# Cross-attention and ternary feed-forward: the first tile's rows in another order, four raw weight pieces, and staging moved

## The chip, the cores and the metric

The kernel runs on one core of a Trainium2 chip. The metric is the device time of one execution in microseconds (us). A core has TensorE (PE; its weight loads are PEld), VectorE (DVE), ScalarE (ACT), GpSimd (POOL), SyncE (SP) and 16 DMA engines. All five run their own instruction streams and meet at semaphores.

## The reference

```python
def layernorm(x): return (x - x.mean(-1)) / sqrt(x.var(-1) + 1e-5)

# x, ctx: (8, 256, 256) f32; mask: (8, 256) int; weights are ternary, -1, 0 or 1, with a scale for each output
def xattn(q, ctx, mask):
    s = einsum('bqd,bkd->bqk', q, ctx) / sqrt(256)
    s = where(causal_upper | (mask == 0), -inf, s)
    return einsum('bqk,bkd->bqd', softmax(s), ctx)

def ffn(x):                                   # tlin(x, w, s) = (x @ w.T) * s
    h = silu(tlin(x, w1, s1)) * tlin(x, w2, s2)   # 256 -> 1024
    h = gelu(tlin(h, h1, sh1))                    # 1024 -> 1024
    h = gelu(tlin(h, h2, sh2))                    # 1024 -> 1024
    return tlin(h, w3, s3)                        # 1024 -> 256

x = x + xattn(layernorm(x), ctx, mask)
x = x + ffn(layernorm(x))
```

## The kernel before

**Tiles.** The 2048 tokens are four tiles of 512 (two batches of 256), a tile is four rows of 128 tokens, numbered 0 to 3; rows 0 and 1 are batch 0. An odd row attends to 256 keys, an even one to 128.

**Arithmetic.** Products in the feed-forward run in F32R, a form of fp32 in which TensorE needs one pass. So that the result stays exact, the activations are split in a high part (`xn_hi`, `h_hi`, rounded to F32R) and a low part (`xn_lo`, `h_lo`), and each weight block is multiplied with both. Weights may run in F32R only if their low 16 bits are zero.

**Weights, pieces and flags.** The weights are 22 pieces of 128 x 1024 f32 (512 KB): 0 to 3 gate and up (two chunks of 128 outputs each), 4 to 11 the first hidden layer, 12 to 19 the second, 20 and 21 the last. A piece is first copied from DRAM to DRAM (`stage`, the form with large packets), then from there to SBUF (`load_piece`). In tile 0, ScalarE sums the low 16 bits of each piece (`test_piece`, L391), TensorE adds the sums over the partitions (`sum_flag`, L968), VectorE writes the flag (`take_flag`, L690), and a `segment` on TensorE reads the flag and runs its products in F32R or in F32. The last flag, LAST, covers pieces 17 to 21. `sum_flag(flag)` waits on TensorE until all tests up to the flag's last piece are done:

```python
pe.wait_ge(low_summed, end)
nc.tensor.matmul(flag_bank(flag), ones[:], low_sums[:, first:end], start=True, stop=True).then_inc(flag_mm, 1)
```

**Raw pieces.** Pieces 0 and 1 are needed too early for the round trip. They are loaded straight into `gate` and `residual` (`load_raw`, L263), tested there, and GpSimd copies them as F32R into `h_hi[1]` (`first_weights`, L366). They are loaded again in the usual way for the later tiles.

**The head.** The first tile's attention has code of its own, row by row, with an order written out by hand on each engine (the lists at the end of each engine's block). Rows are taken as 1, 0, 3, 2 (`FIRST_ROWS`). For each row: statistics of x (VectorE, L615, L620), deviation (L625, or ScalarE L403), turned by TensorE (L1055), copied as queries (L632, L410), scores (L1073) on top of a mask that TensorE has put in the bank (`first_mask_in`, L1063, L1065), maximum (L639), exponentials (ScalarE L417), turned (L1082), copied (L653, L424), attended (L1092), added to x (L666), statistics again, reciprocal square root on GpSimd (`rstd_of`, L337, L338), normalised (L677), turned (L1100), split (ScalarE L430, VectorE L684). `stay_busy` (L1047) issues products whose result is not used.

**The first tile's products.** Gate and up for chunks 0 to 2 are done by batch (256 columns), chunks 3 to 7 in full (512 columns), all at L907. Then the two hidden layers (L928), into which the attention of the next tile is woven, and the last layer (L947). Tiles 1 to 3 follow the same way.

**The queue.** SyncE issues nearly all DMAs of the kernel, in program order, and a wait holds what stands behind it. After the head it alternates `load_piece(n)`, which waits until `stage(n)` has landed, and `stage(n + 2)`.

## Time and profile before

| | |
|---|---|
| median of 3 runs | 376.17 us (375.77 to 377.38) |
| profiled execution | 376.71 us, span 374.6 us |
| TensorE, VectorE, ScalarE, GpSimd busy | 97%, 47%, 40%, 8% of the span |
| DMA | 34.15 MB, 91 GB/s over the span |

The span runs from the first to the last instruction of the profiled execution; its own time is 2.1 us more. Timeline rows give start, duration, engine, line, operation and tiles; where several of one kind follow each other they are merged and the duration is that of the whole stretch. "idle before <- releaser" is how long the engine stood still and what ended it. In the chain of waits each piece of time belongs to the work that the end was waiting for.

### The profile page before, as it was taken

How to read it: one execution, taken by the hardware profiler on the slowest of the kernel's cores; microseconds unless marked ns; L12 is line 12 of the kernel's file. 1: busy time of each engine (PE TensorE's matmuls, PEld its weight loads, DVE VectorE, ACT ScalarE, POOL GpSimd, SP SyncE). 2: the span in 40 equal slices, each digit the busy share in tenths (PEclk: the TensorE clock that was granted, in tenths of full speed). 3: DMA queues.
4: the chain of work that ended last, by engine and by line, in shares of the span. 5: the costliest groups of instructions: out<-in, count | busy, mean ns of one | idle time of the engine just before them, and what ended most of it. 6: DMA issues, size and time to landing. Idle time of an engine off the chain costs nothing.

```text
span 374.6 us, 4879 instructions
## 1 busy us (share of the span) xinstructions
PE 364.7 (97%) x1797; PEld 306.8 (82%) x1797; DVE 176.9 (47%) x406; ACT 149.3 (40%) x252; POOL 28.5 (8%) x50
## 2 busy tenths in 40 slices
PE   8898999999999999999998999999999999999996
PEld 5676888888898888888888888888889888888886
DVE  2747652334565745234564665232456563232324
ACT  3678766593134632262130653235113473122120
POOL 7300031000100022000010004000010000000000
PEclk9999999999999999999999999999999999999999
DMA  7989998981411000000141000000000100000001
GB/s 260 335 288 366 380 401 281 317 274 70 173 40 46 3 2 2 2 0 3 59 139 60 2 1 3 0 2 3 2 0 30 32 3 2 2 2 2 2 2 58
DMA packets 10499, 34.15 MB, mean 91 GB/s; under 512 B 1522, under 2 KB 4468, under 8 KB 10100
## 3 DMA queue, kind: packets, MB, share of 16 engines
q1 hardware_dynamic: 10448, 33.45, 24.9%
q8 instruction: 39, 0.64, 0.7%
q14 instruction: 8, 0.07, 0.1%
q10 hardware_dynamic: 4, 0.00, 0.0%
HBM read 31.34 MB, written 13.63 MB: 120 GB/s over the span
## 4 chain that ended last, share of the span: by engine, by line
PE 93%; issue 2%; ACT 1%; DVE 1%; POOL 1%; DMA 1%; DVEq 0%; ACTq 0%
PE ring L928 62%; PE ring L907 14%; PE ring L947 8%; PE att L858 2%; PE att L877 2%; PE att L848 1%; DMA mask<-in_mask 1%; ACT scaled L391 1%; PE ring L1073 1%; ACT gate L468 1%; PE att L866 1%; PE ring L1055 0%; ACT h_hi L458 0%; PE ring L1092 0%; POOL rstd L338 0%
## 5 line engine op out<-in xcount | busy, mean ns | idle before, releaser
L928 PE MATMUL ring<-h_hi,weights 128*128 128x512 f32 x512 | 201.5, 394 | 0.1
L928 PE MATMUL ring<-h_lo,weights 128*128 128x512 f32 x512 | 199.5, 390 | 0.0
L928 PEld LDWEIGHTS ring<-h_hi,weights 128*128 128x128 f32 x512 | 96.2, 188 | 19.9 <-issue 0.2
L928 PEld LDWEIGHTS ring<-h_lo,weights 128*128 128x128 f32 x512 | 96.2, 188 | 19.7
L480 ACT ACTIVATE act<-ring,scales 128x512 f32<-128x512 f32 x64 | 44.1, 689 | 155.8 <-PE ring L928 155.8
L716 DVE CAST h_hi<-act 128x512 fp32r<-128x512 f32 x64 | 27.3, 427 | 147.9 <-ACT act L480 134.1
L610 DVE TENSOR_TENSOR h_lo<-act,h_hi 128x512 fp32r<-128x512 f32 x96 | 66.2, 689 | 2.6
L907 PE MATMUL ring<-xn_hi,weights 128*128 128x512 f32 x112 | 43.7, 390 | 1.5 <-issue 1.5
L907 PE MATMUL ring<-xn_lo,weights 128*128 128x512 f32 x112 | 43.6, 389 | 0.0
L468 ACT ACTIVATE gate<-ring,scales 128x512 f32<-128x512 f32 x32 | 22.1, 690 | 37.6 <-PE ring L907 37.6
L703 DVE SCALAR_TENSOR_TENSOR act<-ring,scales,gate 128x512 f32<-128x512 f32 x32 | 24.0, 751 | 21.5 <-PE ring L907 17.0
L947 PE MATMUL ring<-weights,h_hi 128*128 128x256 f32 x128 | 31.1, 285 | 0.0
L947 PE MATMUL ring<-weights,h_lo 128*128 128x256 f32 x128 | 30.9, 283 | 0.0
L907 PEld LDWEIGHTS ring<-xn_lo,weights 128*128 128x128 f32 x112 | 21.0, 188 | 5.4 <-issue 1.2
L907 PEld LDWEIGHTS ring<-xn_hi,weights 128*128 128x128 f32 x112 | 21.0, 188 | 4.7 <-issue 0.5
L947 PEld LDWEIGHTS ring<-weights,h_lo 128*128 128x128 f32 x128 | 24.6, 192 | 0.0
L947 PEld LDWEIGHTS ring<-weights,h_hi 128*128 128x128 f32 x128 | 24.6, 192 | 0.0
L391 ACT ACTIVATE scaled<-weights 128x1024 bf16<-128x1024 uint16 x20 | 21.0, 1051 | 1.9 <-DMA weights<-weights_staged 1.5
L458 ACT ACTIVATE h_hi<-act 128x512 fp32r<-128x512 f32 x32 | 20.1, 627 | 1.9 <-DVE act L703 1.9
L337 POOL TENSOR_SCALAR var_eps<-mean_var 128x4 f32<-128x4 f32 (+2 forms) x11 | 2.1, 192 | 244.3 <-DVE mean_var L552 235.2
L729 DVE TENSOR_TENSOR scaled<-ring,down_scale 128x256 f32<-128x256 f32 x16 | 6.8, 422 | 12.0 <-PE ring L947 12.0
L338 POOL TENSOR_TENSOR rstd<-var_eps,minus_half 128x4 f32<-128x4 f32 (+2 forms) x11 | 9.4, 851 | 0.9
(119 smaller groups left out, 243.5 us busy)
## 6 DMA issues: line engine op xcount, KB each, us to landing
weights_staged<-in_weights SPq DMA_DIRECT2D x22, 512.0 KB, 7.0
weights<-weights_staged SPq DMA_DIRECT2D x22, 512.0 KB, 5.6
x_in<-in_x SPq DMA_DIRECT2D x8, 256.0 KB, 2.9
ctx_cols<-in_ctx_cols SPq DMA_DIRECT2D x8, 256.0 KB, 4.3
ctx_rows<-in_ctx_rows SPq DMA_DIRECT2D x4, 512.0 KB, 6.3
out_dram<-residual SPq DMA_DIRECT2D x16, 128.0 KB, 2.2
mask<-in_mask SPq DMA_DIRECT2D x3, 256.0 KB
gate<-in_weights SPq DMA_DIRECT2D x1, 512.0 KB, 5.2
```

Of the source, the lines that this page charges most:

```text
L338: return nc.gpsimd.tensor_tensor(rstd[:, cols], var_eps[:, cols], minus_half[:, cols], op=ALU.pow)
L391: nc.scalar.activation(test_out, low, ACT.Copy, accum_out=low_sums[:, n:n + 1]).then_inc(low_summed, 1)
L458: nc.scalar.activation(h_hi[0][:, c], act32[:, c % 3], ACT.Copy).then_inc(hi_done, 1)
L468: nc.scalar.activation(gate[:, c % 2], ring[2 * c % RING][:], ACT.Silu, scale=gate_scale[:, c:c + 1]).then_inc(gate_done, 1)
L480: nc.scalar.activation(act32[:, n % 3], ring[(2 * HC + HC * layer + c) % RING][:], ACT.Gelu, scale=scale[:, c:c + 1]).then_inc(gelu_done, 1)
L610: nc.vector.tensor_tensor(h_lo[buf][:, c], act32[:, n % 3], h_hi[buf][:, c].bitcast(F32), op=ALU.subtract).then_inc(split, 1)
L703: nc.vector.scalar_tensor_tensor(out=act32[:, c % 3], in0=ring[(2 * c + 1) % RING][:], scalar=up_scale[:, c:c + 1], in1=gate[:, c % 2], op ...
L716: nc.vector.tensor_copy(h_hi[buf][:, c], act32[:, n % 3]).then_inc(hi_made, 1)
L858: ins = nc.tensor.matmul(att[b][:, cols], q_cols[:, b, c, q * P:(q + 1) * P], ctx_cols[:, b, c, 0:(q + 1) * P], start=(c == 0), stop=(c == ...
L907: ins = nc.tensor.matmul(bank[:, toks], w, part[:, k, toks].bitcast(dt), start=(k == 0 and part is xn_hi), stop=(k == EC - 1 and part is x ...
L928: ins = nc.tensor.matmul(bank[:], w, part[:, k].bitcast(dt), start=(k == 0 and part is h_hi[src]), stop=(k == HC - 1 and part is h_lo[src]))
L947: ins = nc.tensor.matmul(bank[:, 0:EMB], part[:, k, r * P:(r + 1) * P].bitcast(dt), w, start=(k == 0 and part is h_hi[0]), stop=(k == last ...
```

## The change

Rows are taken as 0, 1, 2, 3 on all engines. Pieces 2 and 3 are raw as well, loaded into `ctx_cols` (after row 3's scores) and `work` (after row 3's probabilities are turned), and copied by GpSimd into the rest of `h_hi[1]`; their round trips are gone from the head. GpSimd's copies wait for normalised rows. Flags are eight in place of nine: gate and up have two (pieces 0 and 1, 2 and 3), and gate and up run in two segments in place of seven. There are 18 idle products of 256 columns in front and 6 later, where there were 6 of 512 in front and 5 later. The usual loads of pieces 0 and 1 for the later tiles, staged beside pieces 9 and 10 before, are four now, staged beside pieces 17 to 20. The loads of tile 1's keys, mask and values wait for the first hidden product too. In the excerpt, removed lines of the hand-written orders on GpSimd, ScalarE and VectorE are left out.

```diff
 HID2_CHUNKS = ((0, 3), (3, 5), (5, 8))
-GATE_UP_A, GATE_UP_B, GATE_UP_C, HID1A, HID1B, HID1C, HID2A, HID2B, LAST = range(9)
-FLAG_ENDS = (1, 2, 4, 7, 9, 12, 15, 17, PIECES)
+GATE_UP_A, GATE_UP_B, HID1A, HID1B, HID1C, HID2A, HID2B, LAST = range(8)
+FLAG_ENDS = (2, 4, 7, 9, 12, 15, 17, PIECES)
 FLAG_PIECES = tuple(zip((0, *FLAG_ENDS), FLAG_ENDS))
 RING = 6
 CH = 3 * HC
-FIRST_ROWS = (1, 0, 3, 2)
...
-        first_pieces = [h_hi[1][:, 2 * n:2 * n + 2].rearrange("p c t -> p (c t)") for n in range(2)]
-        raw_pieces = [gate[:].rearrange("p n t -> p (n t)"), residual[:].rearrange("p r d -> p (r d)")]
+        first_pieces = [h_hi[1][:, 2 * n:2 * n + 2].rearrange("p c t -> p (c t)") for n in range(GU_P)]
+        raw_pieces = [gate[:].rearrange("p n t -> p (n t)"), residual[:].rearrange("p r d -> p (r d)"),
+                      ctx_cols[:].rearrange("p b c t -> p (b c t)"), work[:]]
         probs_t = turned[:, 0:PAIR * KEYS].rearrange("p (b k) -> p b k", b=PAIR)
         gate_scale, up_scale, h1_scale, h2_scale = (scales[:, n] for n in range(4))
...
         def flag_bank(flag):
             first, end = FLAG_PIECES[flag]
-            if flag in (GATE_UP_A, GATE_UP_B):
-                return ring[4][:, 8 * flag:8 * flag + end - first]
+            if flag == GATE_UP_A:
+                return ring[4][:, 0:end - first]
             if flag <= HID1C:
                 return att[0][:, 0:end - first]
...
             load_queries(0)
             load_keys(0)
             sp.wait_ge(x_loaded[0], 16)
+            load_values(0)
             load_raw(0)
-            load_values(0)
             load_raw(1)
-            stage(2)
+            sp.wait_ge(first_scores[3], 1)
+            load_raw(2)
             sp.dma_start(scales[:], scales_d).then_inc(scales_in, 16)
-            stage(3)
+            stage(GU_P)
+            sp.wait_ge(first_probs_turned[3], 1)
+            load_raw(3)
+            stage(GU_P + 1)
             ahead = 2
-            for n in range(2, PIECES):
+            for n in range(GU_P, PIECES):
                 load_piece(n)
                 if n + ahead < PIECES:
                     stage(n + ahead)
-                if n in (FLAG_PIECES[HID1C][0], FLAG_PIECES[HID1C][0] + 1):
-                    stage(n - FLAG_PIECES[HID1C][0])
+                if FLAG_PIECES[LAST][0] <= n < FLAG_PIECES[LAST][0] + GU_P:
+                    stage(n - FLAG_PIECES[LAST][0])
                 if n == FLAG_PIECES[HID1A][0]:
                     sp.dma_start(down_scale[:], down_scale_d.partition_broadcast(P)).then_inc(down_scale_in, 16)
                 if n == FLAG_PIECES[HID1B][0]:
                     sp.wait_ge(x_attn_done, ROWS)
                     load_queries(1)
                 if n == FLAG_PIECES[HID1C][1] - 1:
+                    sp.wait_ge(hid_mm, 1)
                     load_keys(1)
                     load_mask(1)
                     load_values(1)
-            for n in range(2):
+            for n in range(GU_P):
                 load_piece(n)
             for t in range(TILES - 2):
...
+            def first_rstd_of(b):
+                pool.wait_ge(first_moments, 2 * b + 2)
+                cols = slice(2 * b, 2 * b + 2)
+                chain(rstd_of(cols))
+                nc.gpsimd.tensor_scalar(neg_rstd[:, cols], rstd[:, cols], -1.0, 0.0, ALU.mult, ALU.add
+                                        ).then_inc(first_rstd, 1)
+            def first_attention_rstd(r):
+                pool.wait_ge(first_moments, ROWS + r + 1)
+                rstd_of(slice(r, r + 1)).then_inc(first_rstd, 1)
...
+            first_rstd_of(0)
             first_mask_of(1)
-            first_rstd_of((0, 1), 2)
-            first_rstd_of((2, 3), 4)
-            first_rstd_of((1,), 5)
+            first_rstd_of(1)
             first_weights(0)
-            first_rstd_of((0,), 6)
+            first_attention_rstd(0)
+            first_attention_rstd(1)
+            pool.wait_ge(first_xn[1], 1)
             first_weights(1)
-            first_rstd_of((2, 3), 8)
+            first_attention_rstd(2)
+            first_attention_rstd(3)
+            pool.wait_ge(first_xn[3], 1)
+            first_weights(2)
+            first_weights(3)
             for t in range(1, TILES):
                 make_rstd(t, 0)
...
             act.dma_start(mask[0:1, :, 0:SEQ].bitcast(I32), mask_d[0:1]).then_inc(mask_loaded, 16)
             act.wait_ge(down_free, ROWS)
             load_table(0, ACT.Exp)
+            first_deviation(0)
+            first_deviation(1)
+            first_queries(0)
+            first_deviation(2)
             first_queries(1)
+            first_queries(2)
+            first_exponentials(0)
             first_exponentials(1)
+            first_exponentials(2)
+            first_evacuate_probs(1)
+            first_evacuate_probs(2)
+            first_exponentials(3)
             test_piece(0, raw_pieces[0], raw_in[0])
+            test_piece(1, raw_pieces[1], raw_in[1])
             first_evacuate_probs(3)
+            first_split(0)
             first_split(1)
+            test_piece(2, raw_pieces[2], raw_in[2])
+            test_piece(3, raw_pieces[3], raw_in[3])
+            first_split(2)
+            first_split(3)
             load_table(1, ACT.Silu)
             act.wait_ge(scales_in, 16)
...
             def first_layer(t):
                 for c in range(HC + 1):
+                    if t == 0 and c == 0:
+                        take_flag(GATE_UP_B)
...
                         nc.vector.scalar_tensor_tensor(out=act32[:, c % 3], in0=ring[(2 * c + 1) % RING][:],
                                                        scalar=up_scale[:, c:c + 1], in1=gate[:, c % 2],
                                                        op0=ALU.mult, op1=ALU.mult).then_inc(gated, 1)
-                    if t == 0 and c == 0:
...
                 results(t)
+            nc.vector.memset(h_lo[0][:, 0, 0:SEQ].bitcast(F32), 0.0).then_inc(idle_made, 1)
             nc.vector.memset(zero_col[:], 0.0).then_inc(down_free, ROWS)
             dve.wait_ge(x_loaded[0], 16)
+            first_stats_of(0, x_in)
+            first_moments_of(0, 0)
             first_stats_of(1, x_in)
+            first_moments_of(1, 0)
             dve.wait_ge(x_loaded[1], 16)
+            first_stats_of(2, x_in)
+            first_moments_of(2, 0)
             first_stats_of(3, x_in)
+            first_moments_of(3, 0)
+            first_deviation(3)
+            first_max(0)
+            first_neg_max(0)
+            first_queries(3)
             first_max(1)
+            first_neg_max(1)
+            first_evacuate_probs(0)
+            first_max(2)
+            first_neg_max(2)
+            first_inverse(0)
             first_max(3)
+            first_neg_max(3)
             first_attention(0)
             first_attention_stats(0)
+            first_moments_of(0, 1)
+            first_attention(1)
+            first_inverse(1)
+            first_attention_stats(1)
+            first_moments_of(1, 1)
+            first_attention(2)
+            first_normalise(0)
+            first_normalise(1)
             take_flag(GATE_UP_A)
+            first_attention_stats(2)
+            first_split(0)
+            first_split(1)
+            first_moments_of(2, 1)
             first_attention(3)
             first_attention_stats(3)
+            first_moments_of(3, 1)
+            first_normalise(2)
+            first_normalise(3)
+            first_split(2)
+            first_split(3)
             dve.wait_ge(scales_in, 16)
             tile(0)
...
                 def piece(n):
-                    if t > 0 or n >= 2:
+                    if t > 0:
                         return weights[:, n]
...
-                if flag in (GATE_UP_A, GATE_UP_B):
-                    pe.wait_ge(first_copied, flag + 1)
                 value = pe.value_load(seg_flags[0:1, flag:flag + 1].bitcast(I32), min_val=0, max_val=2**31 - 1)
...
             def first_tile():
-                gate_up = lambda flag, chunks, b=None: segment(flag, lambda dt: gate_and_up(0, chunks, dt, b))
+                def batches(dt):
+                    pe.wait_ge(first_copied, 1)
+                    gate_and_up(0, (0, 1), dt, 0)
+                    first_turn_xn(2)
+                    first_turn_xn(3)
+                    pe.wait_ge(first_copied, 2)
+                    gate_and_up(0, (2,), dt, 0)
+                    gate_and_up(0, (0,), dt, 1)
+                    sum_flag(GATE_UP_B)
+                    gate_and_up(0, (1, 2), dt, 1)
+                    gate_and_up(0, (3,), dt)
+                def remaining(dt):
+                    pe.wait_ge(first_copied, GU_P)
+                    gate_and_up(0, (4, 5, 6), dt)
+                    sum_flag(HID1A)
+                    gate_and_up(0, (7,), dt)
                 hid1 = lambda flag, *chunks: segment(flag, lambda dt: hidden(0, 0, chunks, dt))
                 hid2 = lambda flag, *chunks: segment(flag, lambda dt: hidden(0, 1, chunks, dt))
-                gate_up(GATE_UP_A, (0, 1), 0)
-                first_turn_xn(3)
-                first_turn_xn(2)
-                gate_up(GATE_UP_B, (2,), 0)
-                gate_up(GATE_UP_A, (0, 1), 1)
-                gate_up(GATE_UP_B, (2,), 1)
-                sum_flag(GATE_UP_C)
-                gate_up(GATE_UP_B, (3,))
-                gate_up(GATE_UP_C, (4, 5))
-                sum_flag(HID1A)
-                gate_up(GATE_UP_C, (6, 7))
+                segment(GATE_UP_A, batches)
+                segment(GATE_UP_B, remaining)
                 hid1(HID1A, 0, 1)
                 sum_flag(HID1B)
...
             def stay_busy(n):
                 for _ in range(n):
-                    nc.tensor.matmul(ring[RING - 1][:], h_lo[0][:, 0, 0:P], h_lo[0][:, 0], start=True, stop=True)
+                    nc.tensor.matmul(ring[RING - 1][:, 0:SEQ], h_lo[0][:, 0, 0:P], h_lo[0][:, 0, 0:SEQ], start=True,
+                                     stop=True)
...
+            stay_busy(18)
             pe.wait_ge(ident_made, 1)
             pe.wait_ge(first_consts, 3)
+            first_turn(0)
             first_mask_in(0)
             first_turn(1)
+            first_score(0)
+            first_turn(2)
+            first_turn(3)
+            first_score(1)
             first_mask_in(1)
-            first_turn(0)
-            first_score(1)
-            first_turn(3)
-            first_turn(2)
-            first_score(0)
+            first_turn_probs(0)
+            first_score(2)
             first_score(3)
             first_turn_probs(1)
-            first_score(2)
-            first_turn_probs(0)
             pe.wait_ge(ctx_rows_in, 16)
+            first_attend(0)
+            first_turn_probs(2)
             first_attend(1)
+            first_attend(2)
+            first_turn_probs(3)
+            stay_busy(6)
+            first_turn_xn(0)
             pe.wait_ge(ones_made, 1)
             sum_flag(GATE_UP_A)
-            stay_busy(1)
-            first_turn_probs(3)
-            first_attend(0)
+            first_turn_xn(1)
             first_attend(3)
-            first_turn_probs(2)
-            first_turn_xn(1)
-            first_attend(2)
-            stay_busy(1)
-            sum_flag(GATE_UP_B)
-            first_turn_xn(0)
```

## Rows read from the trace of the kernel before

**Rows 1.** The page, busy time and share of each engine

```profile
PE 364.7 (97%) x1797; PEld 306.8 (82%) x1797; DVE 176.9 (47%) x406; ACT 149.3 (40%) x252; POOL 28.5 (8%) x50
```

**Rows 2.** Chain of waits in order of time, 0 to 130 us: start, us, what

```profile
7.61 1.71 PE ring L1073 x4
...
10.61 0.88 PE att L1073 x4
...
13.71 0.49 DVE x_attn L666
...
15.78 0.99 POOL h_hi L366
...
20.31 2.17 PE ring L907 x16
...
39.10 7.25 PE ring L928 x32
...
66.16 0.12 PE att L968 x2
...
88.17 0.12 PE att L968 x2
```

**Rows 3.** Timeline of TensorE, 0 to 40 us

```profile
1.47 2.93 PE L1047 MATMUL ring<-h_lo 128*128 128x512 f32 x6 [1.47 <-DVE h_lo L783]
4.76 0.36 PE L1063 MATMUL ring<-scaled 1*128 1x256 bf16 x1 [0.36 <-POOL scaled L360]
...
5.57 0.63 PE L1055 MATMUL ring<-ident,work 128*128 128x128 f32 x2
...
9.96 0.65 PE L1073 MATMUL ring<-ctx_cols,turned 128*128 128x128 f32 x4
...
11.53 0.61 PE L1073 MATMUL att<-ctx_cols,turned 128*128 128x128 f32 x4
...
16.97 0.44 PE L1100 MATMUL ring<-ident,act 128*128 128x128 f32 x2 [0.99 <-DVE act L677]
...
34.41 0.39 PE L968 MATMUL att<-low_sums,ones 128*128 128x3 f32 x2 [0.75 <-ACT scaled L391]
...
38.94 0.39 PE L928 MATMUL ring<-h_hi,weights 128*128 128x512 f32 x1
```

**Rows 4.** Windows: us, busy of each engine, clock, DMA share, GB/s

```profile
60.00:80.00 20.00, 20.00 (x97) 16.82 (x95) 5.72 (x19) 12.51 (x24) 0.00 (x0) 1.00 0.90 303
36.00:44.00 8.00, 8.00 (x37) 6.61 (x36) 4.29 (x9) 5.57 (x8) 0.00 (x0) 1.00 1.09 444
```

**Rows 5.** Timeline of SyncE's DMA issues, 0 to 130 us

```profile
12.69 0.51 SPq L251 DMA_DIRECT2D weights_staged<-in_weights  x1
...
18.77 0.33 SPq L255 DMA_DIRECT2D weights<-weights_staged  x1
...
57.59 0.32 SPq L255 DMA_DIRECT2D weights<-weights_staged  x1
...
80.47 0.32 SPq L255 DMA_DIRECT2D weights<-weights_staged  x1
```

**Rows 6.** Timeline of ScalarE, 45 to 115 us, the last piece's test

```profile
84.66 1.05 ACT L391 ACTIVATE scaled<-weights 128x1024 bf16<-128x1024 uint16 x1
85.61 0.19 ACT L391 ACTIVATION_READ_ACCUMULATOR scaled<-weights 128x1 f32 x1
```

**Rows 7.** Timeline of VectorE, 0 to 45 us, the normalisations

```profile
15.88 1.03 DVE L677 TENSOR_SCALAR act<-x_attn,mean_var,rstd 128x256 f32<-128x256 f32 x1
...
17.71 1.10 DVE L677 TENSOR_SCALAR act<-x_attn,mean_var,rstd 128x256 f32<-128x256 f32 x1 [0.21 <-POOL rstd L338]
...
21.91 0.74 DVE L677 TENSOR_SCALAR act<-x_attn,mean_var,rstd 128x256 f32<-128x256 f32 x2 [1.07 <-POOL rstd L338]
```

**Rows 8.** Landing times: load_piece (L255), and the page's DMA issues

```profile
DMA to landing us min/median/max: 3.2/5.6/9.3
...
gate<-in_weights SPq DMA_DIRECT2D x1, 512.0 KB, 5.2
```

More of the change, by code:

```diff
@@ L177, in xattn_ffn @@
         gate_mm = sem("gate_mm")
-        raw_in = [sem(f"raw_in{n}") for n in range(2)]
+        raw_in = [sem(f"raw_in{n}") for n in range(GU_P)]
         first_copied = sem("first_copied")
@@ L343, in make_rstd @@
                 rstd_of(slice(0, ROWS)).then_inc(rstd_ready, 1)
-            def first_rstd_of(rows, count):
-                pool.wait_ge(first_moments, count)
-                cols = slice(min(rows), max(rows) + 1)
-                if count > ROWS:
-                    rstd_of(cols).then_inc(first_rstd, 1)
-                else:
-                    chain(rstd_of(cols))
-                    nc.gpsimd.tensor_scalar(neg_rstd[:, cols], rstd[:, cols], -1.0, 0.0, ALU.mult, ALU.add
-                                            ).then_inc(first_rstd, 1)
+            def first_rstd_of(b):
[7 more added lines that the diff above has]
+                rstd_of(slice(r, r + 1)).then_inc(first_rstd, 1)
             def first_mask_of(b):
@@ L406, in first_queries @@
             def first_queries(r):
-                act.wait_ge(first_turned, FIRST_ROWS.index(r) + 1)
+                act.wait_ge(first_turned, r + 1)
                 b, q = divmod(r, 2)
@@ L640, in first_max, with first_neg_max @@
                                         op=ALU.max).then_inc(first_maxed, 1)
-            def first_neg_max(r, count):
-                dve.wait_ge(first_maxed, count)
+            def first_neg_max(r):
+                dve.wait_ge(first_maxed, r + 1)
+                dve.wait_ge(first_rstd, r // 2 + 1)
                 nc.vector.scalar_tensor_tensor(out=neg_max[:, r:r + 1], in0=row_max[:, r:r + 1], scalar=FLOOR,
@@ L653, in first_evacuate_probs, with first_inverse @@
                 nc.vector.tensor_copy(probs_t[:, r // 2, cols], first_bank[r][:, cols]).then_inc(first_probs_t[r], 1)
-            def first_inverse(rows, count):
-                for r in rows:
+            def first_inverse(b):
+                for r in (2 * b, 2 * b + 1):
                     dve.wait_ge(first_probs[r], 1)
-                cols = slice(min(rows), max(rows) + 1)
+                cols = slice(2 * b, 2 * b + 2)
                 nc.vector.reciprocal(inv_sum[:, cols], row_sum[:, cols]).then_inc(first_inv, 1)
-                dve.wait_ge(first_inv, count)
             def first_attention(r):
                 dve.wait_ge(first_attended[r], 1)
+                dve.wait_ge(first_inv, r // 2 + 1)
                 nc.vector.scalar_tensor_tensor(out=x_attn[:, r], in0=first_bank[r][:, 0:EMB], scalar=inv_sum[:, r:r + 1],
@@ L669, in first_attention_stats, with first_normalise @@
             def first_attention_stats(r):
-                dve.wait_ge(x_attn_done, FIRST_ROWS.index(r) + 1)
+                dve.wait_ge(x_attn_done, r + 1)
                 first_stats_of(r, x_attn)
-            def first_normalise(r, count):
-                dve.wait_ge(first_rstd, count)
+            def first_normalise(r):
+                dve.wait_ge(first_moments, ROWS + r + 1)
+                dve.wait_ge(first_rstd, PAIR + r + 1)
                 nc.vector.tensor_scalar(xn_first[:, r], x_attn[:, r], mean_var[:, r, 0:1], rstd[:, r:r + 1],
@@ L778, in tile @@
                 results(t)
+            nc.vector.memset(h_lo[0][:, 0, 0:SEQ].bitcast(F32), 0.0).then_inc(idle_made, 1)
             nc.vector.memset(zero_col[:], 0.0).then_inc(down_free, ROWS)
-            nc.vector.memset(h_lo[0][:, 0].bitcast(F32), 0.0).then_inc(idle_made, 1)
             dve.wait_ge(x_loaded[0], 16)
+            first_stats_of(0, x_in)
+            first_moments_of(0, 0)
             first_stats_of(1, x_in)
-            first_stats_of(0, x_in)
-            first_moments_of(1, 1)
@@ L822, in _ @@
-            first_attention(2)
-            first_moments_of(3, 7)
-            first_split(0)
-            first_attention_stats(2)
-            first_moments_of(2, 8)
-            take_flag(GATE_UP_B)
-            for r in (3, 2):
-                first_normalise(r, 5)
-            for r in (3, 2):
-                first_split(r)
+            first_moments_of(3, 1)
[3 more added lines that the diff above has]
+            first_split(3)
             dve.wait_ge(scales_in, 16)
@@ L894, in gate_and_up @@
                         pe.wait_ge(xn_split, ROWS + PAIR * t)
-                        for n in range(2):
+                        for n in range(GU_P):
                             pe.wait_ge(loaded[n], 16)
```

57 lines of the change are left out of this document (7 added, 50 removed).

## The prediction

> **What bounds the kernel now.** I read the page's busy shares first: TensorE is busy for 97% of the span [rows 1], so only its first microseconds and its gaps can pay. The chain of waits in order of time then shows where it is not fed [rows 2]: up to 20.31 us the chain runs through row work on every engine, the chunks of gate and up follow, with a stall of 0.75 us in front of a sum of low parts at 34.41 us [rows 3], and from 39.10 us the chain is TensorE in hidden products. Nothing in the diff touches tiles 1 to 3 except the loads ahead of them, so what stands at the last flag sum (88.17 us) decides the end: a shift there is handed through unchanged, since only TensorE's own work follows.
>
> Two of TensorE's levels can be told by the spacing of products of one shape, although the granted clock in the windows is written as 1.00 throughout. The four scores of 256 columns at 7.61 us take 1.71 us, the next such four 0.88 us [rows 2]: a factor of two, so 1.2 GHz up to about 9.96 us and 2.4 GHz from there [rows 3].
>
> The second resource is the DMA queue. From 60 to 80 us it is 90% busy at 303 GB/s with one staging and one load per step; from 36 to 44 us, with a third transfer in each step, it moved 444 GB/s [rows 4]. The loads of pieces 14 and 21 are issued at 57.59 and 80.47 us, so one every 3.3 us [rows 5]. ScalarE's test of the last piece starts at 84.66 us [rows 6], and its sum is used at 88.17 us.
>
> **The head, part by part.** *Idle products.* Six of 512 columns took 2.93 us, the last one's drain within it, so 0.427 us apart. Eighteen of 256 columns are 18 x 0.21 = 3.8 us from about 1.1 us (the memset in front is half as long), ending near 5.0 us, where the first mask product stood at 4.76 us [rows 3]. That costs 0.2 us and closes the gap in front of the rows. Whether the clock comes earlier no row shows. Bounds: as before (9.96 us), or as soon after this uninterrupted start as the 5.2 us that passed between 4.76 and 9.96 us, so 6.3 us. I take 7 us, nearer the second, since TensorE has no gap in front of the rows now. TensorE's turns, masks and scores from 5.0 us are 8.4 us at the slow spacing (four turns at 0.43, which is 0.63 without the last drain, two mask sets at 0.8, the 4.76 to 5.57 us of the first, scores at 1.71 twice and at half of that for the half as wide rows twice). With 2.0 us of it slow and 6.4 halved, and 0.7 us of waits for ScalarE's copies, the last score ends at about 10.9 us (12.4 with the late clock), against 12.14 us for the last score before.
>
> *Rows in order 0, 1, 2, 3.* Row 0 needs half the score columns of row 1, and its chain starts earlier: attention of row 0 is added at about 11.8 us, one turn and one pair of products after the last score, where the first stood at 13.71 us [rows 2]. Deviations, maxima, exponentials and copies are the same instructions in another order; they lie beside TensorE's 5.9 us from 5.0 to 10.9 us, and were that cover gone, each is 0.3 to 0.5 us.
>
> *Weight copies on GpSimd.* Before, the two normalisations took 1.03 and 1.10 us beside copies on GpSimd, the first of which stands in the chain with 0.99 us; two later ones took 0.74 together, 0.37 each [rows 2, 7]. Now the first copy runs while VectorE reads PSUM, at about 9.5 us, and the second waits for row 1's normalisation. Saved: 0.66 + 0.73 = 1.4 us. The reciprocal square roots no longer queue behind a copy of 1.0 us (rows 0 and 1), one more microsecond off the chain at 15.78 us [rows 2]. What is queued behind GpSimd's new waits are the copies of pieces 1 to 3, all needed later than this.
>
> *ScalarE.* The tests of pieces 0 and 1 (1.14 us each) now stand ahead of the copy of row 3's probabilities, and the tests of pieces 2 and 3 ahead of the splits of rows 2 and 3. The first pair is done at about 14.9 us, so that row 3 is attended at 16.3 us, and the splits of rows 0 and 1 are done near 16.4 us. Gate and up start at about 16.6 us, against 20.31 us: 3.7 us earlier.
>
> *Gate and up.* 48 products at 0.12 us (16 took 2.17 us, 0.2 of it drain), 40 at 0.227 us (32 hidden ones took 7.25) and 0.7 us for turns are 15.5 us [rows 2]; before, 18.6 us passed to 38.94 us, 3.1 us more, of it 0.75 us in front of the sum at 34.41 us and the rest at changes of segment and waits [rows 3]. Seven segments become two. Piece 3's raw load is issued after row 3's turn, at 13.3 us, and lands by the 5.2 us of the gate load [rows 8] at 18.5 us; its test ends at 19.7 us and holds the splits of rows 2 and 3, a stall of about 0.8 us. Sum 16.6 + 15.5 + 0.8, and 0.8 for changes: the hidden products start at 33.7 us, 5.2 us earlier (bounds 3.5 and 6.5 by clock and landing). The sums that moved are products of 0.12 us each and stand between products; their reading on VectorE stands where VectorE has nothing else to do.
>
> **The queue behind it.** Piece 4's staging went out at 12.69 us and its load at 18.77 us, with three other transfers around it [rows 5]. Now raw piece 2 leaves at about 10.9 us, staging 4 at 12.3, raw 3 at 13.3, staging 5 at 13.8: loads 4 and 5 go out some 2.2 us earlier than before (bounds 1.0 and 3.0). The round trips of pieces 2 and 3 are gone, but SyncE waits for rows in their stead, with an empty queue from about 10 us. Two stagings move away from pieces 9 and 10 and four come in beside pieces 17 to 20, all in front of the last piece's load: it sees two more transfers. Each is 0.524 MB: 1.18 us at 444 GB/s, 1.73 us at 303 GB/s [rows 4]. I take 1.18, being the rate with three in a step. The two removed give 2.4 us, the four added cost 4.7: the last load lands at 83.7 - 2.2 - 2.4 + 4.7 = 83.8 us, where 83.7 is its issue at 80.47 us plus the shortest landing, 3.2 us [rows 5, 8]. With the test of 1.14 us and the sum, the last flag is there at 85.1 us. TensorE would be there at 88.17 - 5.2 = 83.0 us: it stalls for 2.1 us, and 88.17 - 85.1 = 3.1, taken as 3.0 us, is what is left of 5.2. Ends: 0.7 us (1.0 us early, the two more at 1.73 each) and 4.2 us (3.0 us early, the two at 1.0 each, filling some of the idle tenth).
>
> For the queue the Trainium skill, DMA: Bandwidth & Descriptors, section "Where 436 GB/s comes from", states that about 358 GB/s of HBM bandwidth per core binds transfers between HBM and SBUF; at that a piece would be an estimated 1.46 us, and the gain 2.4 us. The 444 GB/s of this trace stand above that limit.
>
> The flags in between: piece 14 is needed at 66.16 - 5.2 = 61.0 us; its load before went out at 57.59 us, now at 57.59 - 2.2 - 2.4 = 53.0, lands by the median 5.6 us at 58.6 and is tested by 59.9 us [rows 5, 8]. No stall there. Keys, mask and values of tile 1 now wait for the first hidden product (about 37.5 us), their place in the queue is later than that, so nothing. Pieces 0 to 3 must be in by 111 us and are by 92 us.
>
> **Sum.** The profiled execution: span 374.6 us, 376.71 us in all; the median of the three runs is 376.17 us. 376.17 - 3.0 = 373.2 us.
>
> **The rivals.**
> - *The queue has room, no stall at the last flag* (0.15). For: 10% idle in rows 4, and step times did not grow by a whole transfer at pieces 9 and 10. Against: two transfers more at 90% busy must show somewhere. Then 5.2 us less: 371.0 us.
> - *The added stagings cost the slow rate* (0.12): a gain of 0.7 to 1.9, in the middle 1.3: 374.9 us. For: 303 GB/s is what the same stretch moved before. Against: it had only two transfers in a step.
> - *The stall puts the clock down* (0.08). TensorE's longest gap after 10 us is 0.99 us, at full speed afterwards [rows 3]; a gap of 2.1 us is in no row. If the level falls, and comes back only after as long as the 5.2 us from 4.76 to 9.96 us, half of that, 2.6 us, is lost: 375.8 us. The Trainium skill, TensorE: Matmul & The Clock Gate, section "What's actually happening", has the throttled state as the default and lets idleness bring it back, which is this rival's mechanism.
> - *ScalarE's tests hold the head* (0.10). If raw piece 3 lands at 21.5 us instead of 18.5, the splits of rows 2 and 3 wait 3 us longer, TensorE gains only 2.2 us, and that decides: 374.0 us. For it: the load is issued only after row 3's turn.
> - *Slower* (0.05): the last piece lands after 87.0 us. That takes the late clock at the start, raw 3 at 15 us and so no lead in the queue, and four stagings at 1.73 us: 83.7 - 2.4 + 6.9 = 88.2 us, flag at 89.5, 1.3 us later than before; with the clock lost, 2.6 more: 380.1 us. It decides from 87.0 us on.
>
> **How the numbers follow.** The forecast, a stall at the last flag and 1.9 to 4.2 us less, has 0.50; its own range is 372.0 to 374.3 us. To hold 8 in 10 the range takes in the room case, the slow-rate case and ScalarE's: 370.9 to 375.6 us; the clock and the slower case lie above it, and a head that gains more than 5.2 us with room in the queue below it, together under 0.2. 0.5% is 1.9 us, about what a measurement of this kernel can tell from no change. Faster by more: 0.47 of the forecast, 0.15, and 0.08 of ScalarE's case, 0.70. Within it: 0.03, the slow rate 0.12, the clock 0.08 and 0.02, 0.25. Slower 0.05.
>
> **What would show it.** Gate products start near 16.6 us and hidden ones near 33.7; normalisations of rows 0 and 1 take 0.37 us each; the load of piece 4 is issued near 16.6 us; load steps from piece 17 on widen from 3.3 to over 4.5 us; the last flag sum waits for ScalarE's test, and that for its load. The forecast is wrong if the last sum comes without a gap, or if hidden products start after 36.5 us.

## The result

The changed kernel takes 374.26 us (372.4 to 378.1, 20 runs) where the kernel before takes 376.99 us (375.22 to 378.62, 20 runs): a ratio of 0.9937, interval 0.9916 to 0.9957, so faster by 0.6%. 373.2 us was forecast, 3.0 us under the three runs shown; it is 2.7 us less. The profiled execution has a span of 372.0 us, against 374.6 us. Runs more than 1.5% above the fastest of their kernel are left out of the ratios (one of the changed kernel's 20; below, one at most of each version, among them one of the early copy's five that took 939.76 us, for a reason that nothing here shows).

The page's busy shares and the changed kernel's chain [rows 1, 2]:

```profile
PE 363.8 (98%) x1808; PEld 307.5 (83%) x1808; DVE 175.8 (47%) x404; ACT 149.8 (40%) x253; POOL 31.6 (8%) x54
...
PE 79%; DMA 18%; issue 1%; SPq 1%; DVE 1%; ACT 0%
```

TensorE had 93% of the chain before. Now it has 79%, and DMA has 18%. The chain in order of time, from the last scores to the last flag sum, leaves TensorE at 11.18 us and comes back to it at 84.59 us:

```profile
9.85 1.33 PE att L1092 x8
...
11.20 0.33 SPq L263
...
12.04 5.00 DMA weights_staged<-in_weights
...
17.44 6.64 DMA weights_staged<-in_weights
...
67.75 6.76 DMA weights_staged<-in_weights
...
74.53 6.13 DMA weights<-weights_staged
...
80.69 0.02 ACT scaled L403
...
81.84 0.58 ACT act L492
...
82.45 0.44 DVE h_hi L731
...
83.61 0.94 DVE turned L595 x2
...
84.59 0.39 PE att L976 x2
84.98 0.39 issue
85.37 3.92 PE ring L938 x16
```

It is to be read from the bottom. The last sum waited for VectorE's copy of the next tile's probabilities (L595), which stands behind a split that waited for ScalarE's gelu, which stood behind the test of piece 20, which waited for the load of piece 20. From there one staging released the next, down to raw piece 2 (L263), which waits for row 3's scores. In this chain the head releases the queue, and the queue sets the end of the weights: each staging goes out only behind the load two pieces before it, so that a round trip of 5.0 to 9.4 us stands in the chain for every two pieces. How much of that end the head decides, the repeated run below shows.

TensorE's timeline, the rows that answer to [rows 3]:

```profile
1.17 4.21 PE L1065 MATMUL ring<-h_lo 128*128 128x256 f32 x18 [1.17 <-DVE h_lo L796]
...
7.00 0.72 PE L1092 MATMUL ring<-ctx_cols,turned 128*128 128x128 f32 x4
7.56 0.62 PE L1074 MATMUL ring<-ident,work 128*128 128x128 f32 x4
...
17.15 0.36 PE L917 MATMUL ring<-xn_hi,h_hi 128*128 128x256 f32 x1 [0.16 <-DVE xn_lo L699]
...
21.50 0.39 PE L917 MATMUL ring<-xn_hi,h_hi 128*128 128x256 f32 x1 [0.34 <-DVE xn_lo L699]
...
34.30 0.44 PE L938 MATMUL ring<-h_hi,weights 128*128 128x512 f32 x1
...
83.44 0.39 PE L938 MATMUL ring<-h_lo,weights 128*128 128x512 f32 x1
84.59 0.39 PE L976 MATMUL att<-low_sums,ones 128*128 128x5 f32 x2 [0.77 <-DVE turned L595]
85.37 0.49 PE L938 MATMUL ring<-h_hi,weights 128*128 128x512 f32 x1 [0.39 <-issue]
```

Four turns take 0.62 us at 7.56 us where two took 0.63 before: the clock goes up (to 2.4 GHz) between 7.0 and 7.6 us, not at 9.96. Gate starts 3.16 us earlier than before (20.31), the hidden products 4.64 us earlier (38.94). TensorE has its last product in front of the sum at 83.44 us, and stands until 84.59.

The queue, in windows and as issues [rows 4, 5]:

```profile
60.00:80.00 20.00, 19.89 (x98) 16.70 (x98) 6.02 (x20) 13.33 (x26) 0.00 (x0) 1.00 0.99 371
36.00:44.00 8.00, 7.93 (x37) 6.53 (x36) 4.42 (x13) 6.26 (x9) 0.00 (x0) 1.00 0.89 320
```

```profile
11.20 0.33 SPq L263 DMA_DIRECT2D ctx_cols<-in_weights  x1
...
12.04 0.60 SPq L251 DMA_DIRECT2D weights_staged<-in_weights  x1
13.67 0.34 SPq L263 DMA_DIRECT2D work<-in_weights  x1
...
17.06 0.34 SPq L255 DMA_DIRECT2D weights<-weights_staged  x1
...
63.14 0.33 SPq L255 DMA_DIRECT2D weights<-weights_staged  x1
...
78.51 3.73 SPq L255 DMA_DIRECT2D weights<-weights_staged  x5
```

From 60 to 80 us the queue is 99% busy at 371 GB/s (90% and 303 before), so part of what was added went into the idle tenth. From 36 to 44 us, where two stagings moved away, it moves 320 GB/s (444 before). The steps from piece 17 to 21 are (78.51 - 63.14) / 4 = 3.8 us.

### The profile page after: what moved, and what is told of

Same layout as the page of the kernel before. It is cut to its first block, busy times and chain, and to the rows that moved or that the text cites. A ratio compares the mean times of both kernels' runs of the same rounds, so it can differ in the third digit from the quotient of the medians.

```text
span 372.0 us, 4892 instructions
## 1 busy us (share of the span) xinstructions
PE 363.8 (98%) x1808; PEld 307.5 (83%) x1808; DVE 175.8 (47%) x404; ACT 149.8 (40%) x253; POOL 31.6 (8%) x54
## 4 chain that ended last, share of the span: by engine, by line
PE 79%; DMA 18%; issue 1%; SPq 1%; DVE 1%; ACT 0%
PE ring L938 51%; DMA weights_staged<-in_weights 16%; PE ring L917 12%; PE ring L957 8%; PE att L887 2%; DMA weights<-weights_staged 2%; PE att L868 1%; PE att L858 1%; PE ring L1065 1%; SPq L255 1%; PE ring L1092 0%; PE att L1092 0%; PE ring L1074 0%; PE att L876 0%; DVE turned L595 0%
## 5 line engine op out<-in xcount | busy, mean ns | idle before, releaser
L917 PE MATMUL ring<-xn_hi,weights 128*128 128x512 f32 x96 | 37.5, 390 | 1.2 <-issue 1.2
L917 PE MATMUL ring<-xn_lo,weights 128*128 128x512 f32 x96 | 37.4, 389 | 0.0
L720 DVE SCALAR_TENSOR_TENSOR act<-ring,scales,gate 128x512 f32<-128x512 f32 x32 | 24.0, 750 | 18.7 <-PE ring L917 16.8
L403 ACT ACTIVATE scaled<-weights 128x1024 bf16<-128x1024 uint16 x18 | 19.0, 1053 | 8.7 <-DMA weights<-weights_staged 8.3
L917 PEld LDWEIGHTS ring<-xn_hi,weights 128*128 128x128 f32 x96 | 18.0, 188 | 5.0 <-issue 1.4
L917 PEld LDWEIGHTS ring<-xn_lo,weights 128*128 128x128 f32 x96 | 18.0, 188 | 3.7
L917 PE MATMUL ring<-xn_hi,h_hi 128*128 128x256 f32 (+1 forms) x44 | 14.2, 344 | 0.5 <-DVE xn_lo L699 0.5
L917 PE MATMUL ring<-xn_lo,h_hi 128*128 128x256 f32 (+1 forms) x44 | 13.7, 331 | 0.0
```

The source lines that it names most:

```text
L403: nc.scalar.activation(test_out, low, ACT.Copy, accum_out=low_sums[:, n:n + 1]).then_inc(low_summed, 1)
L720: nc.vector.scalar_tensor_tensor(out=act32[:, c % 3], in0=ring[(2 * c + 1) % RING][:], scalar=up_scale[:, c:c + 1], in1=gate[:, c % 2], op ...
L917: ins = nc.tensor.matmul(bank[:, toks], w, part[:, k, toks].bitcast(dt), start=(k == 0 and part is xn_hi), stop=(k == EC - 1 and part is x ...
```

## The experiments

Each was timed beside the kernel before on the same chip; ratios are to it, with their interval.

### The changed kernel again, and its stagings elsewhere

The three runs of this part say whether the added stagings hold the last flag.

> The changed kernel once more, as the measure for the other three of this call. All theories: ratio to the kernel before 0.993, span 372.0 us; hidden products from 34.3 us, a gap of 0.8 us in front of the last flag sum and 0.4 us behind it.

0.9929 (0.9897 to 0.9961), span 373.2 us. Its head was faster than in the profile above: the clock was up from the first turn at 4.89 us on, gate began at 16.12 us. But the test of raw piece 3 starts at 19.08 us (19.23 above) behind a wait of 2.53 us for its landing, and the splits of rows 2 and 3 held TensorE for 1.22 us, so that the hidden products began at 34.15 us. The last sum stood at 85.83 us, 1.2 us later than above, behind the same chain. From SyncE's timeline and TensorE's:

```profile
10.18 0.33 SPq L263 DMA_DIRECT2D ctx_cols<-in_weights  x1
...
79.53 3.96 SPq L255 DMA_DIRECT2D weights<-weights_staged  x5
```

```profile
85.83 0.39 PE L976 MATMUL att<-low_sums,ones 128*128 128x5 f32 x2 [1.15 <-DVE turned L595]
```

Raw piece 2 left 1.0 us earlier than above (10.18 for 11.20), and the load of piece 21 1.0 us later (79.53 for 78.51). So the queue's own time differs by some 2 us between two executions of one program, and how early the head releases it doesn't by itself decide when it ends.

**Behind piece 21.**

```diff
-                if FLAG_PIECES[LAST][0] <= n < FLAG_PIECES[LAST][0] + GU_P:
-                    stage(n - FLAG_PIECES[LAST][0])
...
             for n in range(GU_P):
+                stage(n)
+            for n in range(GU_P):
                 load_piece(n)
```

> The four stagings of pieces 0 to 3 are issued behind the load of piece 21. Theory (the queue holds the last flag): pieces 20 and 21 land two to four us earlier, ScalarE no longer waits 2.07 us in front of the test of piece 20, the gap at the last sum (0.77 us and 0.39 us of restart) goes, span 372.0 - 1.6 = 370.4 us, 0.9957 of the changed kernel. Rival (the order on ScalarE and VectorE holds it: the copy of probabilities stands behind gelu and tests anyway): the gap stays above 0.5 us and the span within 0.4 us of 372.0.

0.9875 (0.9841 to 0.991), 371.85 us, span 369.2 us, which is 1.2 us less than the theory's 370.4. The load of piece 21 leaves at 74.65 us instead of 78.51: 3.2 us a step from piece 17 on, where the changed kernel has 3.8 and 3.7. The product behind the last sum starts 2.63 us earlier (82.74 for 85.37), of it 0.73 us from a head that was faster in this execution (hidden products at 33.57 us). Of ScalarE's timeline, tests of the last pieces come without a wait, and of TensorE's the sum without a gap:

```profile
77.63 1.06 ACT L403 ACTIVATE scaled<-weights 128x1024 bf16<-128x1024 uint16 x1
...
79.26 1.04 ACT L403 ACTIVATE scaled<-weights 128x1024 bf16<-128x1024 uint16 x1
```

```profile
82.59 0.28 PE L976 MATMUL att<-low_sums,ones 128*128 128x5 f32 x2
```

The rival, that the order on ScalarE and VectorE makes the gap, is out: order and tests are the same, and the gap is gone. Measured twice more below, it gave 0.9860 (0.9825 to 0.9895) and 0.9874 (0.9847 to 0.9902). With the early copy below (the same within the intervals) it is the fastest version here, and beats both kernels.

**Beside pieces 9 to 12.**

```diff
-                if FLAG_PIECES[LAST][0] <= n < FLAG_PIECES[LAST][0] + GU_P:
-                    stage(n - FLAG_PIECES[LAST][0])
+                if FLAG_PIECES[HID1C][0] <= n < FLAG_PIECES[HID1C][0] + GU_P:
+                    stage(n - FLAG_PIECES[HID1C][0])
```

> The four stagings stand beside pieces 9 to 12. Theory (each added staging pushes later landings, by about 1.2 us): the load of piece 14 goes out two to four us later than the 54.8 us of the changed kernel, the sum in front of hidden layer 2 (61.4 us) gets a gap of 2 us or more, the last one less; the span is 372.5 to 374 us. Rival (the queue has room, since it moved 371 GB/s instead of 303 in 60 to 80 us when it was given more): no gap over 0.5 us at that sum, span 370.4 to 371 us.

0.999 (0.9962 to 1.0017), span 374.0 us: no gain is left that can be told from none. As the theory had it, the load of piece 14 goes out at 58.12 us instead of 54.80, and two sums stand for tests that stand for loads:

```profile
49.42 0.39 PE L976 MATMUL att<-low_sums,ones 128*128 128x3 f32 x2 [0.78 <-ACT scaled L403]
...
64.39 0.36 PE L976 MATMUL att<-low_sums,ones 128*128 128x3 f32 x2 [2.04 <-ACT scaled L403]
65.34 0.49 PE L938 MATMUL ring<-h_hi,weights 128*128 128x512 f32 x1 [0.59 <-ACT act L492]
```

That is 3.3 us for four stagings against the first profile, but what one staging costs can't be read from one pair: with the same transfers in front of it, the load of piece 14 left at 56.75 us in the repeated run and at 53.28 us in the late staging. So it is 0.3 to 1.2 us each, and the 1.18 us of the forecast is at the upper end. Of the 12 runs here, five have a mean granted clock under 0.999, which adds to the loss; the other seven have a median of 375.69 us, 1.4 us under the kernel before.

### The idle products

```diff
-            stay_busy(18)
+            stay_busy(12)
```

> Twelve idle products in front in place of eighteen, as long as the six wide ones before. Theory (the unbroken start raises the clock early, and the scores release the queue): the products run at the slow spacing until 9 to 10 us in place of 7.2 us, row 3's scores end about 1 us later, gate starts about 1 us later, all loads go out about 1 us later and the span grows by 1 us to 373 us. Rival (the idle products do not matter): the clock rises at the same time, the rows even start 0.4 us earlier, span 371.6 to 372.0 us.

0.9945 (0.9915 to 0.9975), span 374.6 us. Row 1's scores run at the slow spacing as in the kernel before, and so does all up to about 10.6 us:

```profile
1.17 2.93 PE L1065 MATMUL ring<-h_lo 128*128 128x256 f32 x12 [1.17 <-DVE h_lo L796]
...
8.12 1.91 PE L1092 MATMUL ring<-ctx_cols,turned 128*128 128x256 f32 x4
```

Raw piece 2 is issued at 12.41 instead of 11.20 us, gate starts at 18.36, and the last sum at 86.51 us behind a gap of 2.09 us. Between this ratio and the repeated run's lie only 0.16%, less than their intervals. The later end fits a delay handed through the queue to the last flag, but doesn't show it: the load of piece 21 leaves at 79.64 us here and at 79.53 us in the repeated run of the changed kernel, where raw piece 2 left 2.2 us earlier. Without the queue's stall it should show in full:

> Late staging and only twelve idle products in front. Theory (the clock comes later, and TensorE, with no stall at the last flag, hands the whole delay on): the scores run slow until 9 to 10 us, gate starts about 1 us later than in the late staging (16.8 to 17.1 us) and the span is 370.5 to 371 us, 0.989 to 0.990. Rival (the clock's time of rising varies from run to run more than the idle products shift it): the ratio stays at 0.986 to 0.987.

0.9942 (0.992 to 0.9964) beside 0.9874 (0.9847 to 0.9902) for the late staging measured with it: 0.7% for six idle products. Gate starts at 18.30 against 16.63 us, hidden products at 35.08 against 33.45, so 1.6 us are the head's. The rest of this profile's 373.4 - 369.1 = 4.3 us is something else: TensorE stands 2.14 us ahead of tile 2's gate products, and the clock goes down behind that. From its timeline and windows:

```profile
200.29 0.47 PE L917 MATMUL ring<-xn_hi,weights 128*128 128x512 f32 x1 [2.14 <-issue]
...
202.45 0.63 PE L917 MATMUL ring<-xn_lo,weights 128*128 128x512 f32 x1
202.87 0.63 PE L917 MATMUL ring<-xn_hi,weights 128*128 128x512 f32 x1
```

```profile
200.00:202.00 2.00, 1.71 (x6) 1.38 (x7) 0.00 (x0) 0.51 (x1) 0.00 (x0) 0.86 0.21 66
202.00:204.00 2.00, 2.00 (x6) 1.59 (x5) 0.75 (x1) 0.18 (x1) 0.00 (x0) 0.50 0.00 0
204.00:206.00 2.00, 2.00 (x8) 1.60 (x8) 0.17 (x1) 1.18 (x2) 0.00 (x0) 0.79 0.00 0
```

In the late staging's profiles this gap is 0.94 to 1.01 us and the clock stays. The loss is (0.14 + 0.50 + 0.21) x 2 = 1.7 us, and 1.1 us for the longer gap; with the head's 1.6 that makes 4.4 us. 8 of its 12 runs have a mean clock of 0.994 or 0.995; the other four have a median of 373.67 us, 1.9 us or 0.5% over the late staging's 371.78. So about 0.5% are the six idle products (from four runs, 373.29 to 374.69 us), and 0.2% the fallen clock. In the profile of twelve idle products without the late staging the same gap is 1.79 us, 0.6 to 0.7 us over the 1.07 and 1.19 of the changed kernel, and the clock stays up. It also stays up behind that profile's gap at the last flag, 2.09 us and 0.50 us more behind the sum (products 0.23 us apart from 87.69 us on), and behind the 2.04 and 0.59 us of the early staging. So a gap of some 2 us doesn't always put the clock down, and what tells the cases apart is not shown.

### GpSimd's copies

```diff
             first_attention_rstd(0)
+            first_weights(1)
             first_attention_rstd(1)
-            pool.wait_ge(first_xn[1], 1)
-            first_weights(1)
```

> As the late staging, but GpSimd copies piece 1 between the reciprocal square roots of rows 0 and 1, as the kernel before did, without the wait for row 1's normalisation. Theory (a copy on GpSimd holds VectorE's normalisation and the square roots behind it): a normalisation takes 1.0 us or more instead of 0.4, row 1's square root comes about 0.9 us later, gate starts 0.7 to 1.2 us later and so does the end: 0.3% over the late staging. Rival (the tests on ScalarE and the attention of row 3 hold the start of gate anyway, at 15.96 us plus 1.03): gate starts less than 0.3 us later and the end stays.

0.9863 (0.9822 to 0.9904) against 0.9860 (0.9825 to 0.9895) of the late staging (whose expectation was as follows), spans 370.0 and 369.8 us.

> The kernel with the four stagings behind piece 21 once more, as the measure for the copy run of this call. All theories: ratio to the kernel before 0.987, span near 369.5 us, no gap over 0.3 us behind the first hidden product.

Neither theory's size at the start of gate, and at the end the rival's, no difference. The normalisation of row 0 met only the tail of the copy and took 0.67 us, row 1's square root came 0.54 us later (15.04 for 14.50 us), and gate started at 17.63 instead of 17.10 us. By the hidden products 0.23 us were left (34.43 and 34.20), since the wait for piece 3's test took up the rest. So letting the copy wait for row 1's normalisation is worth little in the changed kernel. In the kernel before, where the copies stood in the chain twice, it was another matter:

```diff
+            first_weights(0)
             first_rstd_of((1,), 5)
-            first_weights(0)
             first_rstd_of((0,), 6)
+            pool.wait_ge(first_xn[0], 1)
             first_weights(1)
```

> The kernel before with this part alone: GpSimd copies piece 0 ahead of the square roots and piece 1 after the normalisations of rows 1 and 0. Theory: these two take 0.4 us each in place of 1.03 and 1.10, the square root of row 0 no longer queues behind a copy, gate starts 1.0 to 1.7 us earlier and the end too: 0.9965. Rival (ScalarE's test of piece 1, which ends at 17.3 us, takes their place): gate starts at most 0.5 us earlier, ratio 0.999.

0.9954 (0.9933 to 0.9975), gate at 18.80 us, 1.5 us earlier, span 373.0 us, 1.6 less. VectorE's timeline, for [rows 7]:

```profile
15.71 0.39 DVE L678 TENSOR_SCALAR act<-x_attn,mean_var,rstd 128x256 f32<-128x256 f32 x1
16.83 0.41 DVE L678 TENSOR_SCALAR act<-x_attn,mean_var,rstd 128x256 f32<-128x256 f32 x1
```

### The head's parts in the kernel before

Eighteen products of 256 columns (and the shorter memset) in the kernel before. The later idle products are half as wide and twice as many (not shown in the cut), all else is as it was:

```diff
-            stay_busy(6)
+            stay_busy(18)
```

> The kernel before with this part alone: eighteen idle products of 256 columns in front (from a memset half as long), the later ones of the same total width. Theory: the scores run at the fast spacing from 5 to 7 us instead of 9.96, gate starts 1 to 2 us before 20.31 us, and since that kernel has no wait at its later flag sums the end comes 1 to 2 us earlier: 0.9955. Rival (the chain of rows is held by VectorE and ScalarE, TensorE's speed does not matter): gate starts within 0.4 us of 20.31 and the ratio is 1.000.

0.9956 (0.9932 to 0.9981), gate at 18.28 us, 2.0 us earlier, the hidden products at 36.89 for 38.94, span 371.9 us. The last down product of tile 1 starts 1.46 us earlier (200.39 for 201.85), less than the head's 2.05, and the first gate product of tile 2 2.71 us earlier (200.51 for 203.22), since a gap of the kernel before is not there:

```profile
203.22 0.40 PE L907 MATMUL ring<-xn_hi,weights 128*128 128x512 f32 x1 [1.09 <-issue]
```

So up to 1.1 us of this span's 2.7 are that gap. No releaser is shown for it, and why it comes in one execution and not in another stays open; it is missing in the profile with both parts (below) as well.

Both parts in one kernel (the two diffs above together):

> The kernel before with both parts that paid alone, the idle products (gate at 18.28 us, span 371.9) and the moved copies (18.80 us, 373.0). Theory (these two carry the head's gain, and the new order of rows, the two segments and the raw pieces little): gate starts at 16.8 to 17.3 us, as in the changed kernel, hidden products about 35.4 us as the seven segments stay, and, with no stall at the last flag sum, the span is 371 us: 0.991, no worse than the changed kernel's 0.993. Rival (the two overlap, both fill the same slack, and the row order brings the rest): gate at 18 us or later, span 372 us or more.

> The late staging a third time, as the measure for this call. All theories: 0.986 to 0.988, no gap at the last flag sum.

0.9919 (0.9889 to 0.9949) and 373.08 us; 0.9874 and 371.78 us for the late staging beside it. Spans 371.0 and 369.1 us. The span is the theory's; gate starts at 17.76 us, between the 17.3 us of the theory and the 18 us of its rival: of 2.0 and 1.5 us alone, 2.55 are left together. ScalarE is what is met next: its test of piece 1 runs from 14.97 us, the split of row 1 only behind it.

```profile
14.97 1.05 ACT L392 ACTIVATE scaled<-residual 128x1024 bf16<-128x1024 uint16 x1
15.92 0.19 ACT L392 ACTIVATION_READ_ACCUMULATOR scaled<-residual 128x1 f32 x1
16.01 0.37 ACT L431 ACTIVATE xn_hi<-ring 128x256 fp32r<-128x256 f32 x1
```

The hidden products begin at 36.35 us here and at 33.45 us with the late staging: 1.1 us lie in front of gate (17.76 and 16.63), for which the order of rows and its tests are left (argued: neither was tried alone), and 1.8 us within gate and up (18.6 and 16.8 us), the 0.75 us stall of the sum at 31.83 us among them, which is still there:

```profile
31.83 0.39 PE L968 MATMUL att<-low_sums,ones 128*128 128x3 f32 x2 [0.75 <-ACT scaled L392]
```

So two small edits, without raw pieces and with the old order, come to 0.9919, where the whole change has 0.9937 and 0.9929: within their intervals the same. The whole change with its stagings moved (0.9874) is 0.45% ahead of both.

## Why the prediction was right

**The bound.** A head that gains more than the end does, and the last flag as the place where it is given back, was the forecast, and the trace and the late staging show it: hidden products 4.64 us earlier, the last sum 3.42 us, the end 2.6 us.

**The head.** Last scores at 11.2 us (forecast 10.9), gate at 17.15 (16.6), hidden products at 34.30 (33.7), normalisations 0.40 and 0.41 us (0.37), raw piece 3's test a wait of 1.65 us on ScalarE and 0.34 us on TensorE (0.8). The clock came between 7.0 and 7.6 us (7). That the idle products do it was a choice between two bounds without a row; the runs with twelve, and with eighteen in the kernel before, show it. Whether their number or the closed gap in front of the rows (0.46 us with twelve, none with eighteen) does it, they don't tell apart.

**The queue.** Loads of piece 4 at 17.06 us (16.6). The last piece's test starts at 83.28 us directly behind its landing (83.8). But this term came out by errors that offset each other. The lead of the queue, put at 2.2 us, was 1.7 us at piece 4 and 0.37 at piece 9 (34.72 for 35.09), 1.8 us too little. The two stagings that moved away gave 2.4 us by piece 14 (54.80 for 57.59), as forecast, and 1.1 us more came by piece 17. The four added ones cost 2.0 us of the 3.9 us lead at piece 17 instead of 4.7: steps of 3.8 us where over 4.5 were forecast, against 3.2 us in the late staging, so about 0.6 us each there (0.5 in the repeated run) and not 1.18. And the last load took 4.8 us from its issue to the start of its test (78.51 to 83.28), where the shortest, 3.2 us, was put in. That the head's lead carries through the queue at all is doubtful: over the eight profiles with the changed kernel's queue up to there, the load of piece 14 leaves at 52.87 to 56.75 us, and the latest belongs to the head that released the queue first (10.18 us).

**The stall.** 0.77 us by the profile, plus the sum's start, 0.39 us, behind it, where 2.1 us were forecast. In the two other profiles of that queue order it is 1.15 us (the repeated run) and 2.09 us (twelve idle products). In the first, TensorE came 0.8 us later than forecast (83.8 for 83.0), and the sum 0.5 us earlier. And I had not priced the restart: the sum is 3.42 us earlier than before (88.01 and 84.59 in the timelines), the product behind it 2.78 us (88.15 and 85.37), so 0.64 us go into the restart, in which TensorE reads a flag that it used to have in time. Nor had I named VectorE's copy as releaser: the sum also waits for `probs_evac`, and the test of piece 20 delays that. The test of piece 21 ended at 84.44 us, 0.15 us before the sum, so both waits were due.

**The size.** 3.0 us against 2.7 us of the medians. Part of this closeness is luck. Of the 20 runs, 13 have a mean granted clock of 0.999 or 1.000 and a median of 373.54 us, 3.4 us under the kernel before; the other seven have 0.990 to 0.995 and a median of 376.38 us, 2.8 us longer. The first part is more than the forecast, and the second is a loss that the forecast had only as a rival, at 0.08 and 2.6 us.

**The rivals.** The queue had room for a part (99% busy, 371 GB/s), not for all. The limit of 358 GB/s that the Trainium skill, DMA: Bandwidth & Descriptors, section "Where 436 GB/s comes from", states did not bind: 20 us at 371 GB/s stand above it. The clock did not fall behind this stall: in the profile its windows stay at 1.00. But it can fall, at a gap of 2.14 us in another place, as the run with twelve idle products and late staging showed, and in seven of the 20 runs it was lower somewhere. This rival's premise was misread: the longest gap after 10 us in the kernel before is not 0.99 us but the 1.09 us at 203.22 us, outside [rows 3]. ScalarE's tests hold the head in some executions (1.22 us in the repeated run). Slower did not come.

**What stays open.** Of the runs of the repeated changed kernel, 8 have a granted clock of 1.0 and a median of 373.0 us, 3 have 0.995 and 376.9 us; 27 of the 29 of the kernel before beside it and all 17 of the late staging have 1.0. The one profile with a fallen clock has it at tile 2's start; whether the changed kernel loses it there or behind the last flag's gap no profile of such a run shows. The eight at full clock are only 1.2 us over the late staging's 371.85 us; the rest of the 2.1 us between the medians is the fallen clock. Nor was the order of rows tried by itself, or a third staging kept in flight (`ahead` is 2 everywhere), though the chain is made of such round trips.

## What to carry to other kernels

When a head is made faster, ask which transfers it releases and what their next deadline is: here the order of stagings decided whether a head 4.6 to 5.5 us faster became 2.7 or 5.3 us. Put transfers with a late deadline (needed at 111 us) behind those with an early one, also if the queue looks idle in between. Before a large rearrangement, try the small parts alone: idle products and two moved copies gave as much as the whole as it was first built. And take the price of a transfer from more than one profile: here one and the same load moved by up to 3.9 us between executions.

## What the hardware showed unexpectedly

- The granted clock is written as 1.00 in all windows of the first 10 us, while products are spaced at 0.427 us for 512 columns, nearly twice the later 0.227. The spacing has to be read.
- When the clock rises varies between executions of one head: before 4.9 us, between 7.0 and 7.6 us, and in between; with twelve products or the old six it was between 9.0 and 10.7 us each time seen.
- Gaps of 0.9 to 1.2 us, one of 1.79 us, and two of 2.04 and 2.09 us with another 0.5 to 0.6 us close behind left TensorE's clock up; one of 2.14 us was followed by 1.7 us lost at half speed.
- VectorE's normalisation takes 0.39 to 0.41 us alone and 1.03 to 1.10 us beside a whole copy on GpSimd, 0.67 us beside the tail of one; the copy keeps its 1.03 us.
- A third transfer of 0.524 MB in each step made steps of 3.6 to 3.8 us out of the late staging's 3.2, so it cost 0.4 to 0.6 us, where each of the two others stands for 1.6 us of a step.
